# Zeroing the pad rows of four count tiles on two engines behind the chunk ramp's first operations, and making three Z tiles at earlier chunks

## The reference, cut to what matters

```python
# layer 0, four rounds k over x1 = x @ W1 + b1  (512 wide)
deg   = segment_sum(1, dst);  dis = max(deg, 1) ** -0.5
alpha = tanh(g[dst] @ gw[k][:512] + g[src] @ gw[k][512:] + gb[k])
g     = g + segment_sum(dis[src] * dis[dst] * alpha * g[src], dst)
# layers 1 to 3: mean aggregation, attention, normalised sum
```

## Time and profile before

| | us |
|---|---|
| median of three runs | 1540.82 (1540.71 to 1540.93) |
| the profiled execution, its own time | 1542.8 |
| its span in the trace | 1540.9 |
| TensorE busy | 1515.3 (98%) |
| VectorE busy | 886.8 (58%) |
| ScalarE busy | 750.1 (49%) |
| GpSimd busy | 185.9 (12%) |

### The profile page before, as it was taken

How to read it: one execution, slowest core, us unless ns; L and a number is a source line. 1 busy time by engine, 2 the same in 40 slices (tenths; PEclk the granted TensorE clock), 3 DMA queues, 4 the chain that set the end, 5 groups by cost and what they waited for, 6 DMA issues and landing times.

```text
span 1540.9 us, 19220 instructions
## 1 busy us (share of the span) xinstructions
PE 1515.3 (98%) x6985; PEld 1219.2 (79%) x6985; DVE 886.8 (58%) x1413; ACT 750.1 (49%) x1346; POOL 185.9 (12%) x306
## 2 busy tenths in 40 slices
PE   6999999999999999999999999999999999999997
PEld 5877878878887888788878777888888778877776
DVE  9878888886645343323333343567598356436346
ACT  6577677768733332424332133345696246533232
POOL 0110021324200000000000000212053013100013
PEclk9999999999999999999999999999999999999998
DMA  5333154326774434433344424564466248645345
GB/s 193 109 117 126 34 195 131 98 77 199 262 255 143 157 103 139 136 102 130 114 167 128 147 80 160 195 209 163 148 197 189 99 143 290 187 133 164 92 128 178
DMA packets 103198, 231.75 MB, mean 150 GB/s; under 512 B 23162, under 2 KB 25972, under 8 KB 103096
## 3 DMA queue, kind: packets, MB, share of 16 engines
q1 hardware_dynamic: 89996, 191.54, 39.3%
q10 hardware_dynamic: 13100, 38.86, 6.6%
HBM read 170.98 MB, written 59.37 MB: 149 GB/s over the span
## 4 chain that ended last, share of the span: by engine, by line
PE 93%; DVE 4%; DMA 1%; ACT 1%; issue 1%; SPq 0%; POOL 0%; POOLq 0%; ACTq 0%; DVEq 0%
PE bank L982 17%; PE bank L838 15%; PE bank L840 15%; PE bank L839 15%; PE bank L986 9%; PE bank L984 9%; PE bank L993 8%; PE bank L1071 2%; PE bank L908 1%; DMA out<-R 1%; PE bank L876 1%; DVE oK L1787 1%; ACT Tt L1155 0%; DVE Zl L1510 0%; DVE wl L1431 0%
## 5 line engine op out<-in xcount | busy, mean ns | idle before, releaser
L838 PE MATMUL bank<-wh,xh 128*125 128x512 f32 x1032 | 415.3, 402 | 0.7 <-DVE G L1721 0.7
L839 PE MATMUL bank<-wl,xh 128*125 128x512 f32 x1040 | 410.4, 395 | 0.0
L840 PE MATMUL bank<-wh,xl 128*125 128x512 f32 x1040 | 409.6, 394 | 0.0
L982 PE MATMUL bank<-Zh,Mh 125*125 125x512 f32 x990 | 394.9, 399 | 0.0
L1443 DVE TENSOR_TENSOR xl<-xs,xh 128x1000 fp32r<-128x1000 f32 x130 | 155.4, 1198 | 291.5 <-ACT xh L1120 291.2
L1120 ACT CAST xh<-xs 128x1000 fp32r<-128x1000 f32 x130 | 132.9, 1026 | 304.7 <-PE bank L840 293.1
L993 PE MATMUL bank<-Zl,Mh 125*125 125x512 f32 x590 | 232.5, 394 | 0.0
L840 PEld LDWEIGHTS bank<-wh,xl 128*125 128x125 f32 x1040 | 193.0, 186 | 48.9
L839 PEld LDWEIGHTS bank<-wl,xh 128*125 128x125 f32 x1040 | 193.1, 186 | 44.5
L838 PEld LDWEIGHTS bank<-wh,xh 128*125 128x125 f32 x1032 | 191.1, 185 | 45.5 <-issue 1.0
L982 PEld LDWEIGHTS bank<-Zh,Mh 125*125 125x125 f32 x990 | 183.5, 185 | 44.1
(11 more groups left out here) (186 smaller groups left out, 1826.1 us busy)
## 6 DMA issues: line engine op xcount, KB each, us to landing
xs<-xT_d SPq DMA_DIRECT2D x80, 500.0 KB, 3.6
Ar<-a_d SPq DMA_DIRECT2D x100, 312.5 KB, 3.5
xs<-hT_d SPq DMA_DIRECT2D x40, 500.0 KB, 3.5
x_d<-XO ACTq DMA_DIRECT2D x30, 512.0 KB, 5.1
R<-x_d SPq DMA_DIRECT2D x60, 256.0 KB, 4.2
xT_d<-XT ACTq DMA_DIRECT2D x30, 500.0 KB, 3.9
ws<-in_W SPq DMA_DIRECT2D x30, 256.0 KB, 3.5
Tt<-m_d SPq DMA_DIRECT2D x10, 625.0 KB, 4.2
```

What stands on the lines that cost most here:

```text
L838: te.matmul(o, xh[i % 2][:, k, :], wh[s][:], start=(k == 0), stop=False)
L839: te.matmul(o, xh[i % 2][:, k, :], wl[s][:], start=False, stop=False)
L840: m = te.matmul(o, xl[i % 2][:, k, :], wh[s][:], start=False, stop=(k == 7))
L982: te.matmul(o, Mh[i][:, s, :], zh, start=(n == 0), stop=False)
```

## The change

VectorE clears only the two `AF16` tiles, and does so behind the two operations on `mid`, ahead of `off`; GpSimd clears the two `AT16` tiles behind `half`, on a semaphore of their own. ScalarE writes Zh of tiles 0 and 1 after the turned counts of t = 5 and of tile 2 after t = 6; VectorE writes the Zl of these at chunks 134, 146 and 152. The general path (an `Else`, for edges that are spread wider than these) has one call moved.

```diff
+Z_AT = (134, 146, 152)
...
+        s_padt = sem("s_padt")
...
-                q.wait_ge(s_pad, 6)
+                q.wait_ge(s_pad, 4)
...
-                    q.wait_ge(s_pad, 4)
+                    q.wait_ge(s_padt, 2)
                     ac.activation(AT16[t % 2][0:T, u:w, :], bank[6 + i % 2][0:T, 0:(w - u) * T]
...
                 if t == 1:
-                    q.wait_ge(s_pad, 4)
                     slab_split(q, 5)
...
-                if t == 7:
-                    for d in range(3):
+                if t == 5:
+                    for d in range(2):
                         z_first(d)
+                if t == 6:
+                    z_first(2)
...
                 ve.memset(zz[:], 0.0).then_inc(s_zz, 1)
-
-                for t in AF16 + AT16:
-                    ve.memset(t[96:128, :, :], 0.0).then_inc(s_pad, 1)
                 q.wait_ge(s_pool0, 1)
...
                 chain("v", ve.tensor_scalar(mid[:], mid[:], WHOLE, -WHOLE, ALU.add, ALU.add))
+
+                for t in AF16:
+                    ve.memset(t[96:128, :, :], 0.0).then_inc(s_pad, 1)
                 mine()
                 q.wait_ge(d_edge, 32)
...
-                        if c in (150, 155, 160):
-                            d = (150, 155, 160).index(c)
+                        if c in Z_AT:
+                            d = Z_AT.index(c)
                             z_lower(d, d, G[:, d, :], DIS)
...
             chain("p", po.memset(half[:], -0.5))
             mine()
+            for i, t in enumerate(AT16):
+                po.memset(t[96:128, :, :], 0.0).then_inc(s_padt, 1)
+                q.wait_ge(s_padt, i + 1)
             rsqrt_degrees(0, 5, 1)
```

More of the change, by code:

```diff
@@ L1225, in apply @@
                 q.wait_ge(s_rstd, i + 1)
-                q.wait_ge(s_pad, 8)
+                q.wait_ge(s_pad, 6)
                 if i in (NT, NT + 1):
@@ L1832, in build @@
                                                  ALU.add, ALU.is_equal).then_inc(gS, 1)
+                        if t == 5:
+                            degrees(0, 5)
                         if t < 8:
@@ L1836, in build @@
                             x1_post(t)
-                        if t == 5:
-                            degrees(0, 5)
                         if t == 8:
@@ L2017, in gpsimd_program @@
                         po.memset(t[96:128, :], 0.0).then_inc(s_pad, 1)
-                        q.wait_ge(s_pad, 7 + i)
+                        q.wait_ge(s_pad, 5 + i)
                 if j < NJ:
```

## The result

The kernel after takes 1537.73 us (median of 16 runs, 1537.08 to 1540.51) beside 1541.05 us for the kernel before, measured with it (16 runs, 1540.71 to 1542.99). The ratio is 0.9978, with a 95% interval of 0.9971 to 0.9984: faster by about 3.4 us. The forecast was 3.97 us and 1536.9. The time lies in the range and the way was foreseen. Of the two terms of the sum one was too large (the start) and one too small (the Z tiles), and the two errors partly cancel.

What follows compares the result with a forecast made beforehand. VectorE was taken to bound the kernel to 26.4 us, then TensorE, with a dear `oK` wait at 96.72. 2.62 + 1.35 = 3.97 us off 1540.82 gave 1536.85, rounded to 1536.9 us; range 1536.2 to 1538.3.

Steps and rivals of the forecast that it cites:

- the start: Head of the kernel: two MEMSETs leaving VectorE bring `off` and the work behind it forward by 2.62 us.
- the Z tiles: TensorE's wait for `oK` at 96.72 us goes when Zh and Zl move: 1.35 us.
- Steps 1 and 2: VectorE's start: two MEMSETs and gaps give 2.62 us; `mid` going first moves nothing; `off` starts at 4.45 us.
- Step 3: Edge DMAs ahead of `off`: last packet between 4.0 and 4.1 us, 0.35 us to spare, so no wait.
- Step 4: GpSimd's two MEMSETs: 1.2 us each, done near 4.5 us, 15 us of cover, no cost.
- The rival: Longer GpSimd MEMSETs hold VectorE's TENSOR_SCALARs on `sm` and `hi` by a shared port, 1.6 us; 10% together with late edges.
- Step 5: TensorE up to 26.5 us: makes up its late first product, VectorE stays the bound by 0.3 us, 2.6 us reach it.
- signs of being wrong: `off` behind a DMA; TensorE waiting on `wh` or full from 10 us; idle near chunk 122; gain gone at 1500.
- The first rival: ScalarE or TensorE binds the start, which gives 1.1 to 2.0 us, not 2.6; 1537.4 to 1538.3 us; 16%.
- Step 6: Zl at the new chunks: VectorE loses its 2.41 us wait for Zh, TensorE's whole 1.35 us wait goes, at most.
- The second rival: TensorE's wait at 96.7 us stays or returns a few chunks later; sum 2.6 us, 1538.2 us; 10%.
- Step 7: Zh ahead of `xh` and block 18's evacuation: 1.3 us hidden, 0.9 us of cover at chunk 122's bank, more for `xh`.

Runs made afterwards that it cites:

- experiment 6: Kernel after with both edge DMAs issued on SyncE's queue, none on ScalarE's; 1537.78 us against 1541.11 for the kernel before, ratio 0.9974.
- experiment 7: Kernel after with all four MEMSETs on VectorE, behind `mid`; 1540.19 us against 1541.11 for the kernel before, ratio 0.9993.
- experiment 3: Kernel after with all four MEMSETs on GpSimd, AF16's first; 1538.64 us against 1541.21 for the kernel before, ratio 0.9986.
- Experiment 9: experiment 6 with each MEMSET written as 625 32-bit words, not 1250 of 16; 1537.23 us against 1541.45 for the kernel before, ratio 0.9974.
- experiment 10: Experiment 9 with five of ScalarE's ten zero casts moved behind `xh` and the first `wh`; 1537.43 us against 1541.45 for the kernel before, ratio 0.9974.
- experiment 1: Kernel after with Zh and Zl at their old places, so only the MEMSETs moved; 1538.94 us against 1541.21 for the kernel before, ratio 0.9982.
- Experiment 4: Kernel after with Zl back at chunks 150, 155 and 160, Zh still early; 1537.26 us against 1541.21 for the kernel before, ratio 0.9972.
- experiment 5: Kernel after with five Zh (tiles 0 to 4) at once behind t = 5; 1538.11 us against 1541.11 for the kernel before, ratio 0.9979.
- experiment 2: Kernel before with only the Z tiles (Zh and Zl) moved; 1539.86 us against 1541.21 for the kernel before, ratio 0.9989.
- experiment 8: Kernel after with TensorE's hint of the jump 60 chunks ahead, not 30; 1537.91 us against 1541.11 for the kernel before, ratio 0.9977.

## Why the prediction was right

**Steps 1 and 2, the MEMSETs and `mid`.** Right but for 0.19 us. Step 2 let `mid` start at once and gave its turn no price. But `mid`, now first, waits 0.22 us for the ramp, and the gap of 0.32 us in front of the first MEMSET is there as before, so VectorE is done with its MEMSETs at 4.60 us. Without a wait `off` would start at 4.64 (experiment 6) and not at 4.45; experiment 7 has the turn alone, with 0.19.

**Step 3, the edges: the term that was mis-sized.** It took the last packet on ScalarE's queue, at 4.0 to 4.1 us, for the landing and so saw 0.35 us to spare. In the kernel after the last packet starts between 4.20 and 4.25 us, and the semaphore lets the chain go at 4.96, some 0.7 us behind. So the landing, which the step took for free, costs VectorE a wait of 0.46 us. With the 0.15 us that it is late itself the start gives 2.01 us and not 2.62. The bound that the step worked out beside it (5.5 us, 1.1 us lost) held. The Trainium skill's rule (DMA: Bandwidth & Descriptors, Anatomy of one DMA) is told of GpSimd's path. It had the direction right, a delay behind the last byte, but not the size for this queue: the trace has 0.7 us where it would put 2, and 3.5 us of gain where the sum by it was 2.3. From the issue to the landing it was 4.23 us here; in the other profiles where `off` waited the edges landed between 4.51 and 5.01 us. Experiments 3, 9 and 10 all show the edges as what sets the start once VectorE is free.

**Step 4, GpSimd.** Right: 2.33 us for two against 2.4, done at 4.51 against 4.5, and `hi` at its old 0.24 us. The rival was right in kind; experiment 3 shows it, with 1.01 us, as soon as the MEMSETs reach over `hi`.

**Step 5, how much reaches TensorE.** Right. The first product moved up by only 1.0 us, TensorE made the rest up out of its idle time, and all 2.01 us of `off` were there at 24.5 us. Two of the prediction's own signs of being wrong showed up in part, a wait for `wh` (0.70 us) and a full TensorE from 10 to 16 us, but 0.92 us of idle time was left from 16 to 26.5, and VectorE stayed the bound. The first rival (the start bound by ScalarE or TensorE) did not come: experiment 10 took its cause away and won nothing by it. The 0.3 us of room that the step worked out for a shift of 2.62 us were never tried, as no shift was larger than 2.46.

**Step 6, the Z tiles.** The mechanism was right, and the gain a little more than "the most that this wait can give". By the x1 products of VectorE the gain stands at 2.01 us up to 81 us and at 3.67 behind the last chunk (104.03 before, 100.36 after): 1.66 us, not 1.35. 1.53 of it is the stall as experiment 1 shows it, read from start to start: the step took the bracket of an idle time for its price. The second rival did not come. Experiment 4 adds that the moved Zh is all of it.

**Step 7, ScalarE's Zh.** Right in its outcome: no wait of TensorE near chunk 122. Its reasons were not. It named 0.9 us of cover at the bank and said that `xh` had more; experiment 5 shows `xh` and the `xl` behind it giving way first.

**The sum.** 2.01 + 1.66 = 3.67 us at 104 us, and 3.49 at 120. The 0.2 between them is the jump out of the chunks, 0.95 us of idle time against 0.74. No step had it, and experiments 1, 2, 4 and 8 say that it is not the change's: with some or all of the same edits it was 0.56 to 1.25. What sets it stays open. The profile names the end of `xh` or of G in turn, and neither fits: in experiment 4 the matmul starts at 101.16 us while `xh` runs to 101.48, and G has ended 0.06 to 0.84 us ahead of the matmul in the twelve profiles, so that it can be the least of the gap but not its spread. A hint 30 chunks earlier did not shorten it.

The sum was 3.97 us, so it came 0.5 us too high, and it came that near in part by luck: the start fell short by 0.61 us and the Z tiles gave 0.31 more. Against the 1536.9 us the median is 0.8 us high; another 0.2 of that is the kernel before, which measured 1541.05 beside the kernel after and 1540.82 ahead of the prediction.

**What the medians can tell.** By the trace experiments 4, 6, 9 and 10 win 0.3 to 0.7 us more than the kernel after by 120 us. By the medians their ratios are 0.9972 to 0.9974 against 0.9978, inside one another's intervals. The best that can be said is that they are as fast and, by the mechanism, a little faster. Experiments 4 and 6 together were not tried.

## What to carry to other kernels

When work is taken off the head of a chain, read the landing of every transfer that was never late, and take it from what starts behind it or from another load's time from issue to landing, not from its last packet: here the next limit lay 0.5 us behind the freed place. Read the price of a stall from the start of one operation to the start of the next, and not from its bracket (1.53 us against 1.36). Look at what stands behind a moved operation on its own engine with the smallest gap to its reader (`xh` and `xl`, 0.50 us), not at the reader that has the larger name. And moving short operations to GpSimd was free here as long as they ended before VectorE's TENSOR_SCALAR on `hi`: look at what VectorE does beside them.

## What the runs showed of the hardware

- A TENSOR_SCALAR of VectorE over 125x170 elements stood 1.01 us until a GpSimd MEMSET ended (experiment 3); a TENSOR_TENSOR beside the same MEMSETs, and a TENSOR_SCALAR of one element, did not. The other way round, GpSimd's affine select took 0.40 us beside such a TENSOR_SCALAR and 0.29 beside a MEMSET.
- VectorE's TENSOR_TENSOR of 125x1250 in f32 takes 1.46 us alone and 1.9 to 2.6 us when a TENSOR_TENSOR of GpSimd is already under way; when it starts first, GpSimd's takes 1.57 us and more in place of 1.29. Which of these meetings happen differs from profile to profile.
- A MEMSET's time goes by its elements and not by its bytes: 1250 of int16 take 1.10 us on VectorE and 1.17 on GpSimd, 625 of int32 with the same bytes 0.62 and 0.65. (Experiment 9 also writes the rows through a flat view in place of one of 10x125, which was not tried apart.)
- The same load of 83 KB, issued at 0.73 us by the same engine, landed between 4.71 and 5.01 us in different profiles.
- In five of the twelve profiles, of kernels with and without the change, VectorE idles 0.44 to 2.04 us in front of one and the same operation (at 1531.28 us before), which the profile puts down to no engine. With the meetings of GpSimd and VectorE (0.89 to -0.18, 3.42 to 2.68 and 3.95 to 2.98 us of gain in experiments 7, 8 and 10) this makes one profile's span tell little of a change of 3 us. The same operation at several places along the run tells where a gain was made and where it was lost; at 120 us that is good to the spread of the jump, some 0.4 us to either side, and behind the last chunk to about 0.1 us.
